# Two heads' values as the stationary operand in three attentions, and a slot mixer in groups one step apart

## The reference

```python
x = x + tanh(g_xattn[0]) * L0_xattn(ctx, layernorm(x), mask, ...)   # 4 heads of 64; also attends to x itself
x = x + tanh(g_ffn[0])   * L0_ffn(layernorm(x), ...)                # 8 experts, one for each token
x = x + tanh(g_xattn[1]) * L1_xattn(layernorm(x), ctx, ...)         # 8 heads of 64
x = x + tanh(g_ffn[1])   * L1_ffn(layernorm(x), ...)
x = x + tanh(g_xattn[2]) * L2_xattn(layernorm(x), ctx, ...)         # 4 heads of 64
x = x + tanh(g_ffn[2])   * L2_ffn(layernorm(x), ...)
x = x + tanh(g_xattn[3]) * L3_xattn(layernorm(x), ctx, ...)         # 1 head of 256
x = x + tanh(g_ffn[3])   * L3_ffn(layernorm(x), ...)                # slot mixer
```

## Time and profile before

| what | value |
| --- | --- |
| median of 3 runs | 1642.88 us (1641.58 to 1644.1) |
| the profiled execution | 1643.71 us |
| its span | 1641.5 us |
| mean granted TensorE clock | 0.953 |
| PE busy | 1502.2 us (92%) |
| DVE busy | 899.0 us (55%) |
| ACT busy | 609.0 us (37%) |
| POOL busy | 291.1 us (18%) |

### The profile page before, as it was taken

The page is one execution under the profiler, slowest core; times in us unless marked ns, Lnnn a source line. Parts: engine busy times, 40 slices in busy tenths (PEclk is TensorE's granted clock), DMA queues, the critical chain, the costliest instruction groups (busy, mean ns, idle before and its releaser), DMA issues.

```text
span 1641.5 us, 30315 instructions
## 1 busy us (share of the span) xinstructions
PE 1502.2 (92%) x9070; PEld 1093.7 (67%) x9070; DVE 899.0 (55%) x2901; ACT 609.0 (37%) x1705; POOL 291.1 (18%) x409
## 2 busy tenths in 40 slices
PE   5999999859999979999999989979999999888886
PEld 2666666659999946777777667748777644565664
DVE  4788787632232225545555435656666455555755
ACT  3655555412233224444444423223444001443422
POOL 4555566330000040000000000110000011121000
PEclk9999999859999999999999989989999799998888
DMA  5111115249999830000000000010110100341000
GB/s 137 31 33 37 36 35 184 85 152 316 323 320 328 293 104 19 19 9 18 18 18 18 0 1 13 20 45 28 36 29 17 33 20 25 91 164 43 1 21 20
DMA packets 89654, 128.85 MB, mean 78 GB/s; under 512 B 17362, under 2 KB 74786, under 8 KB 84450
## 3 DMA queue, kind: packets, MB, share of 16 engines
q1 hardware_dynamic: 85954, 123.50, 23.5%
q0 software_dynamic: 2432, 4.34, 0.9%
q10 hardware_dynamic: 1184, 0.01, 0.0%
HBM read 112.87 MB, written 11.67 MB: 76 GB/s over the span
## 4 chain that ended last, share of the span: by engine, by line
PE 75%; DVE 8%; issue 8%; POOL 3%; ACT 3%; DMA 2%; SPq 0%; POOLq 0%; DVEq 0%; ACTq 0%
PE bank L2353 10%; PE bank L2501 9%; PE bank L2710 8%; PE bank L2361 6%; PE bank L2803 6%; PE bank L2469 5%; PE bank L2520 4%; PE bank L2480 4%; PE bank L2724 4%; PE bank L2756 3%; PE bank L2772 3%; PE bank L2442 2%; PE bank L2956 2%; PE bank L2403 1%; DMA work<-in_F_b1c 1%
## 5 line engine op out<-in xcount | busy, mean ns | idle before, releaser
L1620 DVE COPY work<-bank 128x300 f32<-128x300 f32 (+1 forms) x272 | 124.1, 490 | 143.4 <-PE bank L2480 142.1
L2501 PE MATMUL bank<-work 128*100 128x64 f32 (+1 forms) x1760 | 191.4, 260 | 10.4 <-DVE work L1620 8.6
L2501 PEld LDWEIGHTS bank<-work 128*100 128x100 f32 x1760 | 177.1, 171 | 35.4 <-issue 19.0
L1112 ACT ACTIVATE work<-bank,work 100x361 f32<-100x361 f32 (+1 forms) x272 | 158.9, 590 | 53.2 <-DVE work L1611 37.6
L1955 DVE SCALAR_TENSOR_TENSOR work<-bank,work 128x128 f32<-128x128 f32 x160 | 56.1, 351 | 160.4 <-PE bank L2710 148.4
L2710 PE MATMUL bank<-work 128*128 128x128 f32 x1216 | 142.8, 275 | 0.6 <-DMA work<-in_F_b1c 0.6
L2710 PEld LDWEIGHTS bank<-work 128*128 128x128 f32 x1216 | 140.6, 192 | 2.2 <-ACT work L1233 1.2
L1611 DVE TENSOR_REDUCE work<-bank 100x1 f32<-100x361 f32 x208 | 102.0, 529 | 67.0 <-PE bank L2469 64.5
L2480 PEld LDWEIGHTS bank<-ident,work 100*128 100x128 f32 x880 | 90.6, 143 | 43.7 <-issue 22.5
L2480 PE MATMUL bank<-ident,work 100*128 100x100 f32 x880 | 106.0, 254 | 8.5 <-ACT work L1112 8.1
L1233 ACT ACTIVATE work<-bank,work 128x128 f32<-128x128 f32 x160 | 58.8, 368 | 144.0 <-PE bank L2710 138.9
(11 more groups left out here) (343 smaller groups left out, 2767.0 us busy)
## 6 DMA issues: line engine op xcount, KB each, us to landing
work<-in_F_w SPq DMA_DIRECT2D x58, 1024.0 KB, 5.8
work<-in_ctxT SPq DMA_DIRECT2D x64, 180.5 KB, 2.4
work<-context_norms SPq DMA_DIRECT2D x32, 288.0 KB, 3.4
context_norms<-work SPq DMA_DIRECT2D x16, 288.0 KB
work<-in_ctx SPq DMA_DIRECT2D x16, 192.0 KB, 2.8
work<-in_F_b SPq DMA_DIRECT2D x20, 128.0 KB, 6.8
work<-sorted_x SPq DMA_DIRECT2D x20, 128.0 KB, 3.0
sorted_y<-work SPq DMA_DIRECT2D x20, 128.0 KB, 6.2
```

The lines of the kernel that those rows point to most:

```text
L1112: nc.scalar.activation(pr[:, 0:NK], S_bank[k][0:T, 0:NK], ACT.Exp, bias=nmax[k][0:T, :], accum_out=rsum[j][0:T, h:h + 1]).then_inc(s.exped ...
L1620: nc.vector.tensor_copy(PT[k][:, 0:CH, :], PT_bank[k][:, 0:CH * T].rearrange("p (c t) -> p c t", c=CH)).then_inc(s.probs_copied.sem, 1)
L2501: ins = nc.tensor.matmul(to, PT[k][:, c, :], values, start=(c == 0), stop=(c == CH - 1))
```

## The change

**In attentions 0, 1 and 2** the operands of the weighing change places, and two heads are weighed together. The 128 columns of values of a pair of heads are the stationary operand; the turned probabilities of both heads (`PW`, 2 x 100 columns) move. So the output comes out turned: rows 0 to 63 are the first head's columns, rows 64 to 127 the second's, and of the two blocks of 100 columns each half of the rows uses its own. Since tokens now lie along the columns, the reciprocals of the sums must be turned too: for each pair, VectorE writes the reciprocals of the two heads, each repeated over 64 columns (`invert`, into `RW`, 100x128); TensorE turns `RW` behind the second head's probabilities, into the same bank; VectorE copies them (`RT`) after the second copy. VectorE multiplies the output with them for each two pairs (`scale_pairs`), straight into the operand of the product with Wo. `o_turn` and `o_copy` go (in attention 0 the turn and copy of the router's input stay). `project` of batch t - 1 moves to where `o_turn` was. A second head's turn waits for `invert`; the weighing of a pair waits for both copies. In attention 0 the context's statistics are cut in two, with `invert` between them.

**In the slot mixer** the pairs go in four groups of two, a step apart: in step p TensorE does the entering group p, VectorE and ScalarE the cell of group p - 1, and all engines the late part of group p - 2; the last two groups are interleaved at the end. Entering pairs use banks 0 to 3, late ones 4 to 7 (the last group 0 to 3). The folding of weights and `pick` stay, in other places.

Cut to its core:

```diff
+                def invert(t, j, p):
+                    wait_for(dve, s.exped, H * t + 2 * p + 2)
+                    nc.vector.reciprocal(RW[0:T, :].rearrange("p (h w) -> p h w", h=2),
+                                         rsum[j][0:T, 2 * p:2 * p + 2].rearrange("p (h o) -> p h o", o=1).broadcast_to([T, 2, W])
+                                         ).then_inc(s.o_scaled.sem, 1)
...
+                    if h % 2 == 0:
+                        wait_for(dve, s.pv, PAIRS[L] * t + h // 2)
+                    nc.vector.tensor_copy(PW[:, 0:CH, k, :], PT_bank[k][:, 0:CH * T].rearrange("p (c t) -> p c t", c=CH)
+                                          ).then_inc(s.probs_copied.sem, 1)
+                    if h % 2 == 1:
+                        nc.vector.tensor_copy(RT[:, h // 2, :], PT_bank[k][:, CH * T:(CH + 1) * T]).then_inc(s.o_scaled.sem, 1)
+                def scale_pairs(t, g):
+                    wait_for(dve, s.pv, PAIRS[L] * t + 2 * g + 2)
+                    wait_for(dve, s.o_scaled, scaled(L, t, g) - 2)
+                    for r in range(2):
+                        rows = slice(W * r, W * (r + 1))
+                        nc.vector.tensor_tensor(OT[rows, 2 * g:2 * g + 2, :],
+                                                O_bank[rows, 0:4 * T].rearrange("p (m r t) -> p m r t", m=2, r=2)[:, :, r, :],
+                                                RT[rows, 2 * g:2 * g + 2, :], ALU.mult).then_inc(s.o_scaled.sem, 1)
...
                     if two_more:
-                        norms(t + 2, j)
+                        ln_x(t + 2, j)
                     for p in range(PAIRS[L]):
+                        invert(t, j, p)
+                        if two_more and p == 0:
+                            ln_x_norm(t + 2, j)
                         probs_copy(t, j, 2 * p)
                         probs_copy(t, j, 2 * p + 1)
                         if p + 1 < PAIRS[L]:
                             maximum(t, j, 2 * p + 2)
                             maximum(t, j, 2 * p + 3)
+                        if p % 2 == 1 and p + 1 < PAIRS[L]:
+                            scale_pairs(t, p // 2)
                         if p == 0 and started:
                             residual(t - 1, 1 - j)
...
-                    o_scale(t, j)
+                    scale_pairs(t, PAIRS[L] // 2 - 1)
...
                     wait_for(pe, s.exped, n + 1)
                     wait_for(pe, s.probs_copied, n - 1)
+                    if h % 2 == 1:
+                        wait_for(pe, s.o_scaled, inverted(L, t, h // 2))
                     for c in range(CH):
                         ins = nc.tensor.transpose(PT_bank[k][:, c * T:(c + 1) * T], PR[k][0:T, c, :], ident[0:T, 0:T])
+                    if h % 2 == 1:
+                        ins = nc.tensor.transpose(PT_bank[k][:, CH * T:(CH + 1) * T], RW[0:T, :], ident[0:T, 0:T])
...
+                def weigh_pair(t, q, p):
+                    wait_for(pe, s.probs_copied, H * t + 2 * p + 2)
...
                     for c in range(CH):
+                        values = vv0(q)[:, c, P * p:P * (p + 1)] if L == 0 else values_of(L, q, c, p)
+                        ins = nc.tensor.matmul(O_bank[:, 2 * T * (p % 2):2 * T * (p % 2 + 1)], values,
+                                               PW[:, c, :, :].rearrange("p r t -> p (r t)"), start=(c == 0), stop=(c == CH - 1))
...
                     if started:
-                        o_turn(t - 1, 1 - j)
+                        project(t - 1, 1 - j)
...
-                        if p == 0 and started:
-                            project(t - 1, 1 - j)
                         if p == 0 and more:
                             step(t + 1, 1 - j, Q_STEP)
-                        weigh(t, j, 2 * p)
-                        weigh(t, j, 2 * p + 1)
+                        weigh_pair(t, j, p)
```

The order of the slot mixer on TensorE, with `late = p - 2` and `early = p` (`both` and `one` do a stage for both pairs of a group or for one of them, if the group exists):

```diff
+                for p in range(SLOT_GROUPS):
+                    both(s_turn, late)
+                    one(sums, early, 0)
+                    one(alpha_turn, early, 0)
+                    if p == 1:
+                        weights_product()
+                    both(qkv, late)
+                    one(attn, late, 0)
+                    one(sums, early, 1)
+                    one(alpha_turn, early, 1)
+                    one(attn, late, 1)
+                    one(gates_in, early, 0)
+                    both(attn_turn, late)
+                    one(new_in, early, 0)
+                    if p == 1:
+                        weights_mean()
+                    both(comm, late)
+                    one(gates_in, early, 1)
+                    both(y_turn, late)
+                    one(new_in, early, 1)
+                    if p == 0:
+                        weights_turn()
+                    both(values, late)
+                    both(mixed, late)
```

More of the change, by code:

```diff
@@ L521, in pair_buffers @@
             return w
-        pair = [pair_buffers(k) for k in range(2)]
-        SWvpT, UNIT, SBE = area.take(2, D), area.take(T + 1), area.take(2)
+        pair = [pair_buffers(area, k) for k in range(2)]
+        UNIT, SBE, SPARE = area.take(T + 1), area.take(2), area.take(2)
         assert pairs_at + NTOK <= unused_by_3 and area.at <= unused_by_3
@@ new lines, in slot_mixer @@
+                third, last = SLOT_GROUPS - 2, SLOT_GROUPS - 1
+                one(rz_tanh, last, 0)
+                both(slots_copy, third)
+                one(rz_tanh, last, 1)
+                one(n_tanh, last, 0)
+                one(qk_copy, third, 0)
+                one(n_tanh, last, 1)
+                one(qk_copy, third, 1)
+                both(slots_copy, last)
+                both(attn_exp, third)
+                both(qk_copy, last)
+                both(y_copy, third)
+                both(attn_exp, last)
@@ L1391, in slot_mixer @@
+                both(y_copy, last)
                 end(act)
@@ new lines, in slot_mixer @@
+                gru_fixed()
+                for p in range(SLOT_GROUPS):
+                    late, cell, early = p - 2, p - 1, p
+                    one(rz_in, cell, 0)
+                    if p == 1:
+                        pick(3)
+                    one(rz_in, cell, 1)
+                    one(v_done, late, 0)
+                    one(alpha_copy, early, 0)
+                    one(rz_done, cell, 0)
+                    one(v_done, late, 1)
+                    one(masked, late, 0)
+                    one(rz_done, cell, 1)
+                    one(masked, late, 1)
+                    one(alpha_copy, early, 1)
+                    one(slots_new, cell, 0)
+                    both(attn_copy, late)
+                    one(slots_new, cell, 1)
+                    both(y_stats, late)
+                    if p == 0:
@@ new lines, in slot_mixer @@
+                    both(residual, late)
+                third, last = SLOT_GROUPS - 2, SLOT_GROUPS - 1
+                both(rz_in, last)
+                both(rz_done, last)
+                one(slots_new, last, 0)
+                one(v_done, third, 0)
+                one(slots_new, last, 1)
+                one(v_done, third, 1)
+                both(masked, third)
+                both(attn_copy, third)
+                one(v_done, last, 0)
+                both(y_stats, third)
+                one(v_done, last, 1)
@@ L2264, in slot_mixer @@
+                both(masked, last)
+                both(values_done, third)
+                both(attn_copy, last)
+                both(residual, third)
+                both(y_stats, last)
+                both(values_done, last)
+                both(residual, last)
                 end(dve)
@@ L2526, in project @@
+                def project(t, j):
+                    if L == 3:
+                        wait_for(pe, s.o_copied, t + 1)
+                        for m in range(2):
+                            ins = nc.tensor.matmul(R_bank[0:T, 0:D], OT[0:CW[m], m, :], wvo3[0:CW[m], m, :], start=(m == 0), stop=(m == 1))
+                    else:
+                        ins = output(t)
+                    if not (isinstance(t, int) and t == 0):
                         ins = mixture_turn(L, t - 1, R_bank)
@@ new lines, in slot_mixer @@
+                third, last = SLOT_GROUPS - 2, SLOT_GROUPS - 1
+                both(s_turn, third)
+                both(qkv, third)
+                one(attn, third, 0)
+                both(s_turn, last)
+                one(attn, third, 1)
+                one(qkv, last, 0)
+                both(attn_turn, third)
+                one(qkv, last, 1)
+                both(comm, third)
+                one(attn, last, 0)
+                both(y_turn, third)
+                one(attn, last, 1)
+                both(values, third)
@@ L3055, in slot_mixer @@
+                both(attn_turn, last)
+                both(mixed, third)
+                both(comm, last)
+                both(y_turn, last)
+                both(values, last)
+                both(mixed, last)
                 end(pe)
```

432 lines of the change are left out of this document (212 added, 220 removed).

## The result

The changed kernel takes 1691.47 us (median; 1690.54 to 1695.07), the kernel before 1642.23 us in the same runs: ratio 1.0305, 95% interval 1.0289 to 1.032. The profiled execution of after took 1691.69 us (its span is 1689.9), 48.0 us more than the one of before (1643.71). The prediction, 1683 us in a range of 1640 to 1707 and slower with 0.79, held.

What follows compares the result with a forecast made beforehand. TensorE, with 75% of the chain, was taken to bound the kernel, with VectorE nearly full too in attention 0. Terms 25.5 + 17.6 + 18.4 - 3.5 - 18 = +40.0 on 1643.7 gave 1683.7 us (1683 by the median), range 1640 to 1707.

Steps and rivals of the forecast that it cites:

- the term that decides: VectorE's reciprocal of 2 x 64 columns per pair of heads: 1.03 us each, bounds 0.25 and 1.21 us.
- Below 0.34 us the change should be a gain: Rival of cheap reciprocals, priced near a 0.25 us copy: about 1638.5 us in all, not slower; chance 0.14.
- 58 x 0.64: The prediction counted the reciprocal some 58 times on the path, 13 + 13 + 16 + 16.
- Attention 0: VectorE's chain closes the loop; two reciprocals and a copy lengthen it: +1.96 us a batch, 13 batches, +25.5 us.
- its mark: Sign that the forecast is right: in attention 0 VectorE is above 90% busy.
- Attention 1: At a batch's last pair TensorE waits for the reciprocal: +1.1 us a batch, 16 batches, +17.6 us.
- Attention 2: Second pair's reciprocal stands behind the previous batch's residual on VectorE: +1.15 us a batch, 16 batches, +18.4 us.
- The ends: After each attention's last weighing the output's turn and copy go: about 1.2 us, three times, -3.5 us.
- The slot mixer: Work regrouped, not reduced; of 30.8 us that could go at best, -18 us, bounds -5 and -31.
- Its 3/5: Slot mixer: three of the new order's five stretches have another group beside, so 3/5 of 30.8 us goes.
- The weighing's gain: Fewer, wider products on TensorE: 0.05 us less a pair with three chunks, 0.13 with four.

Runs made afterwards that it cites:

- run 3: After with each wide reciprocal made as a reciprocal of 2 columns and a copy repeating them over 128: 1656.67 us, ratio 1.0087.
- run 2: The changed attentions of after with the slot mixer of before: 1712.06 us, ratio 1.0428.
- run 9: After with every wide reciprocal made twice, one after the other: 1847.29 us, ratio 1.1244.

## Why the prediction was right, and where it was off

**The reciprocal** was the term that decides, and it was priced well: 1.03 us predicted, 0.947 measured, with bounds of 0.25 and 1.21. Per column it is 7.4 ns over all, and 6.7 from 64 to 128 columns. The estimate that the prediction worked out from the Trainium skill's page "VectorE: DVE Perf Modes", section "Walkthrough: the 8-slice pipeline in each mode", was 8.33 ns a column; the rows of before were nearer. Below 0.34 us the change should be a gain, said the prediction; at run 3's 0.39 us its sum gives 1683.7 - 58 x 0.64 = 1646.6 us. Run 3 took 1656.67, 10 us more; the terms of attentions 1 and 2, below, were too low.

**Attention 0** (24.3 us with its end, 18.3 measured): in the middle of the loop a batch grew to 20.6 us, 20.7 predicted; at its start and end batches grew by 1.1 us at most, and I had charged all 13 alike. The mechanism was right, its mark was not: VectorE was to be over 90% busy and is 17.37 of 20.60 us, 84%, hardly more than the 83% of before. Its timeline shows why:

```profile
261.96 1.06 DVE L1673 COPY work<-bank 128x400 f32<-128x400 f32 x2
262.94 0.25 DVE L1676 COPY work<-bank 128x100 f32<-128x100 f32 x1
...
264.83 0.76 DVE L1684 TENSOR_TENSOR work<-bank,work 64x200 f32<-64x200 f32 x2 [1.39 <-PE bank L2603]
266.36 0.70 DVE L1645 CUSTOM_DVE_ANT_0 bank<-bank,work 100x512 f32<-100x512 f32 x1 [0.77 <-PE bank L2564]
```

From 245.75 to 263.4 its one rest above 0.1 us is of 0.30; then it waits for the weighing and for the next scores, as TensorE had waited for it. The loop closes over both engines, as the prediction said, and so neither is full.

**Attention 1** (16.4 us with its end, 29.4 measured) is the largest miss. The wait is the one predicted, at the predicted pair and of the predicted size (1.01 to 1.02 us of idle time a batch). What was missed is this.

- The work of a steady batch. It was to gain 0.05 us a pair in the weighing and to have the same number of turns. From start to start, the weighing takes 4.49 us a batch for 4.37, and the four turns of the reciprocals 0.62 for 0.38 of the four turns of the output. The 0.179 us for 200 columns, an interpolation, was not too low (0.169 from start to start). But the first product of a pair takes 0.27 us to the second one, its load beginning only with it. So a pair took 1.12 us and not 1.07, against 1.11 in before.
- The first batch: 5.1 us longer (33.9 for 28.8 from its first scores to those of the second). Pair 0 has no weighing ahead of it there to hide its reciprocal, and those of pairs 2 and 3 stand behind the adding back of the experts' rows on VectorE (1.55 us each, from 635.0 and 640.8).
- The last batch: 3.5 us longer, since nothing is projected beside it.

The last two are seen in TensorE's timeline, first batch and then last:

```profile
619.00 0.45 PE L2577 MATMUL bank<-ident,work 100*128 100x100 f32 x3 [1.14 <-DVE work L1657]
...
637.67 0.45 PE L2577 MATMUL bank<-ident,work 100*128 100x100 f32 x3 [1.54 <-DVE work L1657]
643.47 0.45 PE L2577 MATMUL bank<-ident,work 100*128 100x100 f32 x3 [1.70 <-DVE work L1657]
...
983.65 0.45 PE L2577 MATMUL bank<-ident,work 100*128 100x100 f32 x3 [0.60 <-DVE work L1657]
988.98 0.45 PE L2577 MATMUL bank<-ident,work 100*128 100x100 f32 x3 [2.23 <-DVE work L1657]
995.07 0.45 PE L2577 MATMUL bank<-ident,work 100*128 100x100 f32 x3 [1.67 <-DVE work L1657]
```

In run 2, with the same code, the first batch has the same three waits, and yet it is only 1.6 us longer than before (30.4). What differs is the wait before its first weighing, where VectorE waits for GpSimd's norm behind ten gathers of experts' rows: TensorE idles 3.83 us there in after, 1.91 in run 2 and 4.58 in before. The clock differs too, and so the split of the 5.1 us isn't shown.

**Attention 2** (17.2 us with its end, 20.7 measured): 12.71 us a batch, 12.6 predicted, with the wait of 0.90 at the second turn. The rest is the last batch, 1.8 us longer where its end was to make it shorter.

**The ends** were to gain 1.2 us each, and the step itself does: in attention 1 the output product begins 0.86 us after the last weighing's end, 2.17 in before. But only attention 0's last batch gets shorter (3.5 us from its first scores to the experts); in attentions 1 and 2 the last batch's own waits, above, outweigh it.

**The slot mixer** (-18, measured -19.2): the busy time fell by 10.3 us with the clock, the idle time by 8.9, both as the prediction had it; neither bound, 5 or 31, came near. Its 3/5 was a count of stretches that no run tests, so that it came within 1.2 us may be luck.

**By sum:** of the 48.4 us, 53.3 are idle time in the attentions (predicted, with the ends, 13 x 2.09 + 16 x 1.16 + 16 x 1.25 - 3.5 = 62.2), 15.1 are busy time there (the weighing was to give 4.2 back), -19.2 the slots (-18), and -0.8 the rest. Most of the 15.1 comes with the waits: a product counts as busy until its end, 0.16 us after the next one could start, and TensorE's gaps above 0.1 us in the three attentions grew from 60 to 122, which makes 10 us (an estimate). The misses partly cancel, which is luck: attention 0 came out 6.0 us under its term, attentions 1 and 2 13.0 and 3.5 us over theirs. The weighing's gain was not there at all, and the prediction had said of it that the change may also free nothing on TensorE.

## What to carry to other kernels

An operation priced by the column should run on the few numbers that it needs and be repeated by a copy: 0.39 us for 0.95 here. A result that is needed late should be waited for late: moving the wait behind the copies and the weighing made the three attentions 39 us shorter (27 of them TensorE's idle time) with the same work. A product's price should be read from start to start: busy time over the count made 200 columns look nearly as dear as 256 (0.215 and 0.227 us, but 0.169 and 0.216 from start to start). And before a cover is spent, see how much of it is left: of the 64 pairs of attention 1, 44 showed no idle time before a reciprocal of 0.95 us (20 waits in after; a batch's third pair had no cover left, as run 3 shows), and 13 none before two (51 waits in run 9).

## What the runs showed that I had not expected

Waits that recur may be paid for twice: in run 9, where they doubled, the granted clock of attention 1 was 0.92 in place of 0.98, and the same instructions took 26 us more. That the waits brought the clock down is read from the two standing together; nothing was run that changes the one without the other. Some 5 of the 26 us need no clock: 30 more gaps, each with the end of a product before it (an estimate, 0.16 us each).

A product's price goes with its stationary operand as well as its moving one. From start to start at full granted clock, products with 128 stationary columns take 112 ns for 8, 100 and 128 moving columns alike; with 100 stationary columns they take 88 ns for 8 and for 64 moving ones, and with 96, 85 ns for 100. With more moving columns these set the price: 169 ns for 200, 216 for 256, 335 for 400. The weight load takes 168 ns with 100 columns and 190 to 192 with 128. The Trainium skill, page "TensorE: Matmul & The Clock Gate", section "LDWEIGHTS (loading the stationary operand)", says that a load's time goes by the operand's columns, at 1/1.2 ns each; for 28 columns more that is 23 ns (an estimate by that page). The traces agree: 22 to 24 ns more for the load, and 24 for the product.
